# Three banks for the transposed scores, results used a piece later, and VectorE's side pieces moved behind the first scan

## The reference, cut to what matters

```python
x = x + tanh(g_xattn[0]) * L0_xattn(layernorm(x), ctx, ctx, ...)   # CoPE: "core" here, "tail" its output
x = x + tanh(g_ffn[0])   * L0_ffn(layernorm(x), ...)               # experts: "ffn"
x = x + tanh(g_xattn[1]) * L1_xattn(layernorm(x), ctx, ...)        # "cross"
x = x + tanh(g_ffn[1])   * L1_ffn(layernorm(x), ...)               # "gated"

def cope(query, attn_logits, pos_emb):
    gates = sigmoid(attn_logits)
    pos = minimum(flip(cumsum(flip(gates))), 63)
    logits_int = einsum('bhqd,dn->bhqn', query, pos_emb)
    w = pos - floor(pos)
    return take(logits_int, ceil(pos)) * w + take(logits_int, floor(pos)) * (1 - w)
```

## Time and profile before

| what | us |
|---|---|
| median of 3 runs | 5371.37 |
| lowest, highest | 5370.37, 5384.88 |
| the profiled execution, its own time | 5382.85 |
| its span, first to last instruction | 5381.1 |
| VectorE busy | 3956.2 |
| TensorE busy | 3448.0 |
| ScalarE busy | 2431.1 |
| GpSimd busy | 1386.8 |
| mean granted TensorE clock | 0.710 of full speed |

### The profile page before, as it was taken

The page is one execution under the profiler, slowest core; times in us unless marked ns, Lnnn a source line. Parts: engine busy times, 40 slices in busy tenths (PEclk is TensorE's granted clock), DMA queues, the critical chain, the costliest instruction groups (busy, mean ns, idle before and its releaser), DMA issues.

```text
span 5381.1 us, 64444 instructions
## 1 busy us (share of the span) xinstructions
PE 3448.0 (64%) x21126; PEld 2230.8 (41%) x21126; DVE 3956.2 (74%) x8619; ACT 2431.1 (45%) x5441; POOL 1386.8 (26%) x1125
## 2 busy tenths in 40 slices
PE   3447575665757667575665757667575665757576
PEld 2225253443525335253443625335353443525353
DVE  3688686786867768686786867778687776867753
ACT  2454444444444444444444444444444454444432
POOL 0342223223222222223223222222222222222300
PEclk7558686776857768586776857768686776857777
DMA  4000000000000000000000000000000000000000
GB/s 122 8 5 1 3 9 1 11 1 10 1 1 11 1 10 1 3 9 1 11 1 10 1 1 11 1 10 1 2 9 1 11 1 10 1 1 7 1 7 3
DMA packets 42690, 40.91 MB, mean 8 GB/s; under 512 B 6468, under 2 KB 42342, under 8 KB 42360
## 3 DMA queue, kind: packets, MB, share of 16 engines
q1 hardware_dynamic: 42360, 36.85, 2.2%
HBM read 32.64 MB, written 4.19 MB: 7 GB/s over the span
## 4 chain that ended last, share of the span: by engine, by line
DVE 37%; PE 35%; ACT 12%; issue 11%; POOL 2%; POOLq 0%; ACTq 0%; DVEq 0%; DMA 0%; SPq 0%
PE banks L786 6%; DVE banks L710 5%; DVE row_negmax L1220 5%; PE banks L355 5%; PE banks L264 4%; PE banks L286 4%; DVE masks L701 3%; PE banks L799 3%; DVE steps L726 3%; PE banks L319 3%; DVE u L937 2%; DVE c L672 2%; PE banks L1088 2%; PE banks L277 2%; DVE eg_eth L955 2%
## 5 line engine op out<-in xcount | busy, mean ns | idle before, releaser
L710 DVE COPY_PREDICATED banks<-masks,banks 128x448 f32<-128x448 int16 (+5 forms) x1536 | 1029.4, 670 | 31.7
L615 POOL TENSOR_TENSOR steps<-slope,rises 128x512 f32<-128x512 f32 x256 | 303.0, 1183 | 2900.4 <-DVE masks L701 2524.2
L786 PE MATMUL banks<-xn,w 128*128 128x256 f16 x6912 | 878.7, 288 | 167.7 <-ACT h L858 165.4
L786 PEld LDWEIGHTS banks<-xn,w 128*128 128x128 f16 x6912 | 700.3, 104 | 342.1 <-ACT h L858 195.2
L701 DVE TENSOR_SCALAR masks<-shift 128x512 int16<-128x512 int16 x1536 | 335.0, 289 | 473.1 <-ACT shift L543 469.2
L582 ACT ACTIVATE core_pT<-banks 128x512 f32<-128x512 f32 x256 | 152.9, 597 | 616.7 <-PE banks L264 616.1
L799 PE MATMUL banks<-w,a 128*128 128x256 f32 x1152 | 326.4, 434 | 141.7 <-DVE o L964 141.7
L629 POOL TENSOR_TENSOR partial<-partial,core_scores 128x512 f32<-128x512 f32 x256 | 350.6, 1369 | 0.1
L1220 DVE TENSOR_REDUCE row_negmax<-banks 128x4 f32<-128x1024 f32 x256 | 302.9, 1219 | 58.4 <-PE banks L340 58.4
L672 DVE TENSOR_TENSOR_SCAN c<-gate,cap 128x514 f32<-128x514 f32 x256 | 342.0, 1336 | 1.1 <-ACT gate L527 1.1
L1088 PE MATMUL banks<-eg_eth,h 64*128 64x256 f16 x1024 | 253.2, 367 | 127.5 <-ACT a L1155 85.2
(11 more groups left out here) (262 smaller groups left out, 7349.4 us busy)
## 6 DMA issues: line engine op xcount, KB each, us to landing
stage<-in_L_ffn_w SPq DMA_DIRECT2D x16, 512.0 KB, 5.5
ahead<-in_ctx SPq DMA_DIRECT2D x32, 128.0 KB, 2.3
ahead<-in_x SPq DMA_DIRECT2D x32, 128.0 KB, 2.3
u<-in_ctx SPq DMA_DIRECT2D x32, 128.0 KB
x<-in_x SPq DMA_DIRECT2D x32, 128.0 KB
out<-x SPq DMA_DIRECT2D x32, 128.0 KB, 1.8
stage<-in_L_ffn_w SPq DMA_DIRECT2D x8, 256.0 KB, 6.1
stage<-in_L_ffn_sw SPq DMA_DIRECT2D x2, 512.0 KB, 4.5
```

Source lines behind the costliest of these rows:

```text
L710: move = nc.vector.copy_predicated(tab[:, :, 0:S - b], k.masks[:, n, :, 0:S - b], tab[:, :, b:S])
L786: last = nc.tensor.matmul(k.bank[bank][:, f * S:(f + 1) * S], w[:, e, a, c, par, f * P:(f + 1) * P], k.x_parts[:, b, c, :], start=(n == 0) ...
```

## The change

It has three parts. VectorE's side pieces all stand behind the first scan of head s + 1, and `some_pieces` is gone. The transposed scores go to banks 5, 6 and 7 in turn, the value products of all four groups share the two halves of bank 4, and ScalarE copies each quarter of oH to SBUF on the way. Several pieces are split so that a product is used in a later piece than the one that makes it; with them a batch has 110 pieces, and new weights give the counts 4, 3, 4, 4, 3, 4, 4, 6, 19, 10, 4, 4, 11, 16, 10, 4 from slot 3 on. The ahead pieces start a slot later (slot 5), and the copy of core_v is one of its own.

```diff
-PIECE_TIMES = [4] * (4 + 2 * NE) + [2] * 2 + 2 * ([6] * 4 + [0.5] * (H + 1) + [1.2] * (H + 1) + [5] * 3)
+PHASES = [0.5] * (H + 1) + [1.4] * (H + 1)
+PIECE_TIMES = [4] * (4 + 2 * NE) + [2] * 2 + [6] * 4 + PHASES + [5] * 3 + [3.5] * 7 + PHASES + [4] * 4
-AHEAD = [1, 0, 0, 1, 2] + [1] * (H - 5)
+AHEAD = [1, 1, 0, 1, 1, 2] + [1] * (H - 6)
-    return AHEAD[s % H] if s >= 4 and s < G + 4 else 0
+    return AHEAD[s % H] if s >= 5 and s < G + 5 else 0
...
     yield
-    for _ in range(9):
+    for _ in range(10):
         yield
     dve.wait_ge(sem["core_v_psum"], b + 1)
     nc.vector.tensor_copy(k.core_v[:, :, 0:D], k.bank[2][:].rearrange("p (t n) -> p t n", t=NT))\
...
                 if b > 1:
                     moved = step(move, wait=False)
-                    some_pieces(pieces, n)
                 else:
                     move.then_inc(sem["core_moved"], 1)
-        else:
-            for n in range(len(MOVES) - 1):
-                some_pieces(pieces, n)
         if s + 1 < G:
             scan(s + 1)
-        some_pieces(pieces, len(MOVES) - 1)
+        for _ in range(pieces):
+            next(side)
...
     yield
+    yield
     dve.wait_ge(sem["tail_y_done"], at["tail_y_done"] + 1)
     dve.wait_ge(sem["loads"], at["loads"] + 16 * 2 * NT)
     add_to_x(nc, k, step, k.bank[7], k.tanh_g[:, 0:1], k.bo_cope)
-    yield
     norm_vector(nc, k, dve, step, k.norm, "ffn_", at)
...
+    yield
     accumulate(NE - 1)
...
+    yield
     pe.wait_ge(sem[p + "xn_ready"], at[p + "xn_ready"] + NT)
     transpose_tokens(nc, k, k.bank[4], n.xn).then_inc(sem[p + "xT_psum"], 1)
-    yield
     pe.wait_ge(sem[p + "xT_ready"], at[p + "xT_ready"] + 1)
...
     if kind == "gated":
+        yield
+        key_stacks()
+        yield
+        yield
         pe.wait_ge(sem[p + "q_done"], at[p + "q_done"] + 1)
         transpose_tokens(nc, k, k.bank[4], k.qn).then_inc(sem[p + "qT_psum"], 1)
+    else:
+        key_stacks()
...
     def weigh_values(g):
         pe.wait_ge(sem[p + "pT_ready"], at[p + "pT_ready"] + 4 * g + 4)
-        weigh_four(nc, k.v, HD + 1, k.pT, g, k.bank[4 + g // 2], g % 2).then_inc(sem[p + "pv_done"], 1)
+        if g >= 2:
+            pe.wait_ge(sem[p + "oH_ready"], at[p + "oH_ready"] + g - 1)
+        weigh_four(nc, k.v, HD + 1, k.pT, g, k.bank[4], g % 2).then_inc(sem[p + "pv_done"], 1)
...
-        if h >= 2:
-            pe.wait_ge(sem[p + "pT_ready"], at[p + "pT_ready"] + h - 1)
+        if h >= 3:
+            pe.wait_ge(sem[p + "pT_ready"], at[p + "pT_ready"] + h - 2)
         n, r = stack_of(h)
         for c in range(NT):
-            out = k.bank[6 + h % 2][:, c * S:(c + 1) * S]
+            out = k.bank[5 + h % 3][:, c * S:(c + 1) * S]
...
+    def values(g):
+        act.wait_ge(sem[p + "pv_done"], at[p + "pv_done"] + g + 1)
+        nc.scalar.activation(k.oH[:, g, :], k.bank[4][:, g % 2 * S:(g % 2 + 1) * S], ACT.Copy)\
+            .then_inc(sem[p + "oH_ready"], 1)
...
+        if h >= 6 and h % 4 == 2:
+            values((h - 6) // 4)
+        yield
+    values(H // 4 - 1)
...
-    if kind == "cross":
-        dve.wait_ge(sem[p + "q_first"], at[p + "q_first"] + NC)
-        second_part(nc, k.bank[7], w.bq, k.q_parts, sem[p + "q_second"])
     yield
     if kind == "gated":
+        yield
         heads = k.qn.rearrange("p t (h d) -> p (t h) d", d=HD)
         dve.wait_ge(sem[p + "rnorm_ready"], at[p + "rnorm_ready"] + 1)
...
+        yield
         dve.wait_ge(sem[p + "q_first"], at[p + "q_first"] + NC)
         second_part(nc, k.bank[4], None, k.q_parts, sem[p + "q_second"])
+    else:
+        dve.wait_ge(sem[p + "q_first"], at[p + "q_first"] + NC)
+        second_part(nc, k.bank[7], w.bq, k.q_parts, sem[p + "q_second"])
```

More of the change, by code:

```diff
@@ L91 @@
     "cross_maxT_psum": 1, "cross_maxT_ready": 1, "cross_scoresT": 16, "cross_pT_ready": 16, "cross_pv_done": 4,
-    "cross_oH_ready": 2, "cross_heads_psum": 2, "cross_o_ready": 2, "cross_oT_psum": 1, "cross_oT_ready": 1,
+    "cross_oH_ready": 4, "cross_heads_psum": 2, "cross_o_ready": 2, "cross_oT_psum": 1, "cross_oT_ready": 1,
     "cross_y_done": 1, "gated_var_ready": 1, "gated_rstd_ready": 1, "gated_xn_ready": 2, "gated_xT_psum": 1,
@@ L97 @@
     "gated_max_ready": 9, "gated_maxT_psum": 1, "gated_maxT_ready": 1, "gated_scoresT": 16, "gated_pT_ready": 16,
-    "gated_pv_done": 4, "gated_oH_ready": 2, "gated_heads_psum": 2, "gated_o_ready": 2, "gated_oT_psum": 1,
+    "gated_pv_done": 4, "gated_oH_ready": 4, "gated_heads_psum": 2, "gated_o_ready": 2, "gated_oT_psum": 1,
     "gated_oT_ready": 1, "gated_y_done": 1, "gated_norm_ready": 1, "gated_rnorm_ready": 1, "gated_q_done": 1,
@@ L599, in ahead_pool @@
     norm_pool(nc, k, pool, k.core_norm, "core_", raised_by(b))
-    for _ in range(14):
+    for _ in range(15):
         yield
@@ L681, in rises @@
             .then_inc(sem["core_rises"], 1)
-    def some_pieces(pieces, n):
-        for _ in range((n + 1) * pieces // len(MOVES) - n * pieces // len(MOVES)):
-            next(side)
     def head_sums(b):
@@ L903, in side_pool @@
                 .then_inc(k.sem[p + "rnorm_ready"], 1)
-        for _ in range(3 + 2 * H + 5):
+        for _ in range((5 if kind == "gated" else 3) + 2 * H + (6 if kind == "gated" else 5)):
             yield
@@ L1031, in keys_and_values, with key_stacks @@
         token_projection(nc, w.wv, src, k.bank[6]).then_inc(sem[p + "v_psum"], 1)
+    def key_stacks():
+        pe.wait_ge(sem[p + "k_second"], at[p + "k_second"] + NC)
+        pe.wait_ge(sem[p + "v_ready"], at[p + "v_ready"] + 1)
+        for m in range(P // HB):
+            if m >= 2:
+                pe.wait_ge(sem[p + "k_stack"], at[p + "k_stack"] + m - 1)
+            stack_pair(nc, k, 1, k.k_parts, m, k.bank[5 + m % 2]).then_inc(sem[p + "k_stack_psum"], 1)
     if kind == "cross":
         keys_and_values(k.ctxT)
+    yield
     pe.wait_ge(sem[p + "xn_ready"], at[p + "xn_ready"] + NT)
     transpose_tokens(nc, k, k.bank[4], n.xn).then_inc(sem[p + "xT_psum"], 1)
-    yield
     pe.wait_ge(sem[p + "xT_ready"], at[p + "xT_ready"] + 1)
@@ L1096, in attention_tensor @@
     yield
-    pe.wait_ge(sem[p + "oH_ready"], at[p + "oH_ready"] + 2)
+    pe.wait_ge(sem[p + "oH_ready"], at[p + "oH_ready"] + H // 4)
     for t in range(NT):
@@ L1112, in attention_tensor @@
     yield
+    if kind == "gated":
+        yield
 def attention_scalar(nc, k, act, kind, at):
@@ L1121, in keys, with key_stacks @@
         first_part(nc, k.bank[5], w.bk, k.k_parts, sem[p + "k_first"])
+    def key_stacks():
+        for m in range(P // HB):
+            copy_stacks(nc, act, m, k.bank[5 + m % 2], k.keys, sem[p + "k_stack_psum"], sem[p + "k_stack"],
+                        at[p + "k_stack_psum"])
     if kind == "cross":
         keys()
+    yield
     act.wait_ge(sem[p + "xT_psum"], at[p + "xT_psum"] + 1)
     nc.scalar.activation(whole(k.norm.xT), k.bank[4][:], ACT.Copy).then_inc(sem[p + "xT_ready"], 1)
-    yield
     if kind == "gated":
@@ L1133, in attention_scalar @@
     yield
-    for m in range(P // HB):
-        copy_stacks(nc, act, m, k.bank[5 + m % 2], k.keys, sem[p + "k_stack_psum"], sem[p + "k_stack"],
-                    at[p + "k_stack_psum"])
     if kind == "gated":
+        yield
+        key_stacks()
+        yield
+        yield
         act.wait_ge(sem[p + "qT_psum"], at[p + "qT_psum"] + 1)
         first_part(nc, k.bank[4], None, k.q_parts, sem[p + "q_first"])
+    else:
+        key_stacks()
     yield
     for m in range(P // HB):
-        copy_stacks(nc, act, m, k.bank[7 - 3 * (m % 2)], k.queries, sem[p + "q_stack_psum"], sem[p + "q_stack"],
-                    at[p + "q_stack_psum"])
+        copy_stacks(nc, act, m, k.bank[7 - 3 * (m % 2)], k.queries, sem[p + "q_stack_psum"],
+                    sem[p + "q_stack"], at[p + "q_stack_psum"])
     yield
@@ L1154, in attention_scalar @@
             act.wait_ge(sem[p + "pv_done"], at[p + "pv_done"] + (h - RING) // 4 + 1)
-        nc.scalar.activation(whole(k.pT[h % RING]), k.bank[6 + h % 2][:], ACT.Exp, scale=INV_SQRT_HD)\
+        nc.scalar.activation(whole(k.pT[h % RING]), k.bank[5 + h % 3][:], ACT.Exp, scale=INV_SQRT_HD)\
             .then_inc(sem[p + "pT_ready"], 1)
+        if h >= 6 and h % 4 == 2:
+            values((h - 6) // 4)
         yield
[L1158 to L1161, removed]
+    values(H // 4 - 1)
     yield
```

## The result

The changed kernel takes 5652.39 us (median of 4 runs, 5645.83 to 5657.26) against 5371.19: a ratio of 1.0516, 95% interval 1.0494 to 1.0537. It is 5.2% slower; the forecast was 5750 us, 7% slower.

A forecast was written before the change was run, and what follows sets the result against it. VectorE's own work bounds only slots 6 and 7; other stretches are chains across engines. Stretches grow 3.1, 0.5, 9.5 and 13.1 us, +26 a batch, +388 in all, less 10: about 5750 us; forecast 5600 to 5850 (0.62), range 5450 to 5900.

The forecast's parts named there:

- The covers: VectorE's waits between side pieces, filled by copies or the scan, become idle: 1.2 us between gate and linear piece, for example.
- signs named: Among them: first scan near 1.84 us, L955 and L958 near 0.69, slots 14, 15 and 0 over 24 us, clock below 0.71.
- Contention: VectorE against GpSimd's products: 129 us freed on side pieces (86 and at most 43), 119 us lost on the first scan.
- rival 2: Freed contention at L955, L958 and L1205 to L1208, 129 us, decides: about 5300 us; chance 0.07.
- the batch that I took for before: One batch of 16 slots from the middle of the earlier trace, 320.88 us in four stretches, the base for the sums.
- the sum of slots 8 to 2: Slots 8 to 13 grow by 9.5 us, 14 to 2 by 13.1; chains over three engines at an uncertain clock.
- third bank: ScalarE's exponentials gain up to 0.63 us in two heads, 10 us a batch; about half taken, inside the slots.
- rival 4: TensorE's clock falls: above 5850 us; chance 0.10.
- An empty piece takes no time: Using a product a piece later leaves both pieces in one slot, so no latency shrinks.

The follow-up runs named there:

- The move alone: The kernel before with `some_pieces` taken out and all side pieces behind the first scan, nothing else changed: 5761.69 us, ratio 1.0699.
- early lump: The changed kernel with all side pieces behind the second copy, and the other four copies and the first scan behind them: 5705.54 us, ratio 1.0601.
- kernel with two banks: The changed kernel with the transposed scores in banks 6 and 7 by turns, all else as changed: 5729.08 us, ratio 1.0631.
- spread kernel: The changed kernel with `some_pieces` back, so VectorE's side pieces are spread over the copies again: 5249.93 us, ratio 0.9748.

## Why the prediction was right, and where it was off

**The covers** were the main cause, as forecast. The move alone costs 377 us; the loss sits in the slots whose pieces wait; and in slot 3 the early lump keeps both waits although it takes away the late start and the long scan. With the collision of the first scan taken away, 321 of the 402 us are left. The single latencies came out as worked out: slot 3 23.75 (23.6, though its terms add up to 23.7), slot 5 23.35 (23.4), slot 10 18.3 (18.5), slot 14 24.8 (25.1), slot 15 23.8 (24.4), slot 0 24.1 (24.7). Of the signs named, two missed: slot 15 was to be over 24 us, and the mean clock below 0.71.

**Contention.** Both terms are right in size: 84.5 us freed on the two long products (86), 40 on the three of the gated queries (43 at most), 126.6 us more in the first scan (119). The Trainium skill (SBUF — State Buffer, Who interferes with whom) says that the port pair which VectorE and GpSimd share is an exclusive lock. The trace agrees: the scan takes 1831 ns beside the product and 1221 with the product cut short. That freed contention decides (rival 2) is refuted by the move alone.

**What was off** is the size: 388 us of growth from slot 19 to 255 was forecast, and it was 283. 25 of the 105 us come of the batch that I took for before, which was shorter than the mean. The other 80 are the sum of slots 8 to 2, the step that I named as the weakest: +22.6 us a batch forecast, +16.9 measured, while slots 3 to 7 were right in sum (+3.6 and +3.9), by some luck: slot 4 was 1.2 too long (23.1, measured 21.9) and slot 6 as much too short. The term is the score phases. The third bank gave 4.5 us a batch in the mean, about the half of 10 that I took, but it is not in my sum. I wrote that half of the third bank's gain was "inside the slots below", but what I wrote for slots 11 and 12 (25.4 and 18.3) is what two banks take (25.6 and 18.6); with three they take 23.4 and 16.4. Slot 1 was forecast at 20.5 with TensorE at its clock of before, 0.58 of full speed there; it has one head fewer and was granted 0.76: 17.4 us. These three are 7.0 us too long in the forecast; slots 8, 9 and 2 were too short by 0.7, 1.4 and 0.6, and the other slots make up the rest.

**TensorE's clock** did not fall in the mean. I expected a mean below 0.710; it is 0.712, with 0.83, 0.92, 0.67 and 0.60 in the stretches against 0.80, 0.96, 0.71 and 0.60. It was lower by 0.04 in two of the four stretches and higher by 0.03 in one, and no run prices that; in time rival 4 fell. The 0.96 that I gave for slots 4 to 8 stands in the earlier trace rows for slots 6 and 7 alone. The Trainium skill (TensorE: Matmul & The Clock Gate, HAM oscillation — how this bites in real kernels) says that gaps between bursts of matmuls put the array back to the slow clock. In the mean that did not become a cost of this change (0.710 and 0.712), but a single slot's length goes with the clock: slot 1 of the kernel with two banks takes 20.9 us at 0.50 and 16.8 at 0.80.

**"An empty piece takes no time"** was my reason to book nothing for the later pieces. But what a later piece is worth depends on what stands in the gap: with the pieces spread, the new cut and counts are worth 96 us. Two pairs of runs put a figure to the difference. All new pieces, core_v and the ahead pieces included, are worth 66 us spread (5316.10 to 5249.93, with three banks), but 33 behind the scan (5761.69 to 5729.08, with two; this pair has the value products in one bank and the quarter copies between it as well, so the 33 is rough). An empty piece between producer and consumer pulls a copy into the wait. In slot 3 of the spread kernel three copies stand in the wait for the projection and 3.64 us are left of it:

```profile
2562.11 2.12 DVE L713 COPY_PREDICATED banks<-masks,banks 128x496 f32<-128x496 int16 x3
2567.86 0.75 DVE L1021 SCALAR_TENSOR_TENSOR x<-banks,tanh_g,x 128x512 f32<-128x512 f32 x1 [3.64 <-PE banks L287]
```

So the two parts of the change work against each other: the cut makes room for the core's work between a product and its use, and the move takes that work away.

What stays open: why the later core_v and ahead pieces cost 30 us with the old cut, though they end the 2.89 us wait; no run separates the two. No run shows why slot 1 is granted the higher clock either.

## What to carry to other kernels

Independent work on an in-order engine is worth the most between an instruction that feeds another engine and the one that needs the answer. Collecting it ahead of or behind a chain left the busy time here nearly as it was and laid bare the waits that the work had covered; before moving it, list the waits that stand beside it and what they would be without it. A split into more pieces paid more here with other work scheduled into the gap (66 us) than without (33). And contention is a price in busy time. To avoid it paid where the engine hardly waits (slots 5 to 7 here, 36 us by a shift of two copies), and for an instruction that stands ahead of all the waits, as the first scan does in the changed kernel: 145 us of time for 155 us of busy time.

## What was not expected of the hardware

One GpSimd product of 128 x 512 cost 63 us (1.2%) in the spread kernel and 145 us in the changed one, though GpSimd is busy a quarter of the span: its price is the VectorE instruction that stands beside it. With that product short, the scan fell from 1831 to 1221 ns in the changed kernel, and in the spread one L962 fell from 988 to 692.

The same slot of one kernel, with the same instructions, took from 16.8 to 20.9 us in different batches of one execution, with TensorE's granted clock at 0.80 and at 0.50 of full speed.
